# A two-stage kernel on one core: the norms and the first four MLP features moved from between the stages into the scan bodies and the second MLP chunk

## The chip, the core and the metric

One core of a Trainium2 chip runs the kernel. The engines are TensorE (PE, with its weight load PEld), VectorE (DVE), ScalarE (ACT), GpSimd (POOL) and SyncE (SP), which here only issues DMAs. Each has its own queue, taken in order, and they wait for one another by semaphores. The metric is the device time of one execution in microseconds.

## The reference

Input x is (4, 128, 128, 128): four images of 128 channels and 16384 positions.

```python
# layer 0: group norm, layer norm, Mamba over 16384 positions, residual
x1 = x + swap(mamba(layernorm(gn(x)), ...))     # W_in, conv of 4 taps, silu, delta = softplus, scan over
                                                # 16 states per channel (256 channels), y*silu(z), W_out
# layer 1, on the group norm of x1
f = lrelu(sw1 @ gn(x1) + sb1)   # 128 -> 64
f = lrelu(sw2 @ f + sb2)        # 64 -> 32
f = sw3 @ f + sb3               # 32 -> 16
# for each of 128 depth points: the 16 features and the point go through 17 -> 32 -> 32 -> 16 -> 1
sdf = sigmoid(mw4 @ lrelu(mw3 @ lrelu(mw2 @ lrelu(mw1 @ [f, point]))))   # (4, 128, 128, 128)
out = x1 + sdf
```

The group norm has 32 groups of 4 channels and takes mean and variance over whole images, so layer 1's norm of an image needs all of that image's x1.

## The kernel before

An image is cut into T = 32 tiles of L = 512 positions, NT = 128 tiles in all. All data is float32.

**Scan stage.** Loop `layer0(i)`, a "body" for each tile i from 0 to 127, and one more, number 128, that only finishes tile 127. A body has 16 units m, each a group of states. On each engine the body is a hand-written order over m:
- TensorE: `spread` of unit m + 2 (L510), which waits for the scan of unit m; at fixed m also the z, convolution and centring matmuls of tiles i + 1 and i + 2; `add_states` 0 to 2 at m = 7, 9, 12 (L521) and the fourth in the next body at m = 1; `project_out` of tile i - 1 at m = 8 (L534).
- ScalarE: `decay` of unit m + 2 (L811, Exp, two passes), `keep_last` (L815), at fixed m the silus, softplus and copies for tile i + 1; at m = 15 `diagonals` (L801, 16 passes).
- VectorE: `scan` of unit m (L1094, two passes); `gate` of tile i - 1's second half at m = 3 (L1102, L1105), of tile i's first half at m = 12; `residual` of tile i - 1 at m = 11 (L1110 and its statistics L1112); `aggregate1` of an image's statistics (L1116).
- GpSimd: `times_c` of unit m (L942), the product with C, and three diagonal tiles.
- SP: replicates C (L307) and delta (L316) over partitions, loads x, stores x1 (L289).

The group norm of the next image is worked into bodies 27, 28 and 29 of the first three images (GN_MEAN, GN_VAR, GN_SHIFT): TensorE matmuls of one column at m = 5, before `add_states` 0, which then waits for VectorE or ScalarE to have read them; VectorE's `group_dev` (L1043 to L1046) at m = 6, `group_weights` (L1051, L1053) at m = 2 and `group_bias` at m = 6; ScalarE's `group_rstd` (L722, L724) at m = 6. Image 3 has no such steps, as no image follows it.

**Between the stages.** After body 128 come, one after the other: `group_norms1` on TensorE and VectorE and `group_rstds1` on ScalarE (norms of all four images' x1); then for f = 1 to 4 the feature steps: `first_layer` for two pairs of 512-wide tiles (TensorE L620, ScalarE L868), `second_layer` (L626, L873), `third_layer` (L631), `spread_g` on VectorE (L1150, L1151). All of them use one PSUM bank, `f_ps`, so that each waits for the one before. SP loads the tiles of x1 for a feature (L354).

**MLP stage.** Loop `layer1(n)` over 128 "chunks", each of 8 steps k: `leaky1` on VectorE (L1159, 128 x 2048) makes t1 two steps ahead from g; `mm2` on TensorE (L642), `leaky2` on ScalarE (L880), for k = 1, 3, 5 partly on VectorE (L1167, L1169); `mm3` (L653), `leaky3` (L886), `mm4` (L663); a sigmoid per chunk on ScalarE (L891) at k = 3 of the next chunk; the sum with x1 on VectorE (L1176) and the store. Features 5 to 32 are made inside the chunks, one in four chunks. `leaky1` of chunk 0 waits for g of f = 4:

```python
if n % DEPTHS == 0 and k == 0:
    dve.wait_ge(s_g, GQ * (s + 1) + 1)
```

## Time and profile before

| | |
|---|---|
| runs | 9304.48, 9296.48, 9299.93 us, median 9299.93 |
| profiled execution | 9299.72 us, its span 9297.9 us |
| PE busy | 8821.4 us, 95% |
| DVE busy | 8554.3 us, 92% |
| ACT busy | 8027.6 us, 86% |
| POOL busy | 5789.4 us, 62% (all of it in the scan stage) |
| scan stage | to about 5946 us |
| MLP stage | from about 6000 us |

Busy times are of the whole span. Matmuls are pipelined, so a busy PE is not PE at its peak. PEclk is the TensorE clock that was granted, as a share of 2.4 GHz; its levels are 1 (2.4 GHz) and 0.5 (1.2 GHz). A row of the timeline has the start and the length in us, the engine, the line, the operation, its operands, how many instructions are merged in it, and in brackets the idle time before it and what ended it.

### The profile page before, as it was taken

The page shows a single profiled execution, that of the slowest core. Times are in us where ns is not written, and L with a number is a line of the kernel's source. Part 1 is how long each engine was busy: PE and PEld are TensorE (multiplying, and loading weights), DVE is VectorE, ACT ScalarE, POOL GpSimd, SP SyncE. Part 2 cuts the span into 40 slices and gives each one's busy share as a digit, 9 for nine tenths or more (in the row PEclk, how much of TensorE's full clock was granted, in tenths as well). Part 3 has the DMA queues.
Part 4 walks back from the last instruction along what each step waited for, and adds up shares of the span by engine and source line. Part 5 has one row for each costly group of instructions (what it writes and reads, how often), then busy time and mean ns, then how long its engine had stood idle before and what let it go on. Part 6 is the DMA issues. An engine that isn't in the chain of part 4 may idle for free. (4 is left out here: it accounts for less than half of the span.)

```text
span 9297.9 us, 445960 instructions
## 1 busy us (share of the span) xinstructions
PE 8821.4 (95%) x199690; PEld 3709.6 (40%) x199690; DVE 8554.3 (92%) x7167; ACT 8027.6 (86%) x12777; POOL 5789.4 (62%) x2582
## 2 busy tenths in 40 slices
PE   7999999999999999999999999799999999999999
PEld 4555555555555555555555555322222222222211
DVE  7999999999999999999999999799999999999998
ACT  6888888888888888888888888599999999999999
POOL 6999999999999999999999999500000000000000
PEclk9999999999999999999999999899999999999999
DMA  4333333333333333333333333211111111111100
GB/s 118 97 95 90 84 83 88 96 100 95 84 86 80 100 95 95 85 86 79 86 85 85 87 86 85 62 34 34 32 32 35 34 32 34 34 32 32 32 23 19
DMA packets 394196, 638.79 MB, mean 69 GB/s; under 512 B 97872, under 2 KB 98610, under 8 KB 391778
## 3 DMA queue, kind: packets, MB, share of 16 engines
q1 hardware_dynamic: 389184, 608.56, 25.0%
q8 instruction: 1577, 25.84, 1.2%
q14 instruction: 329, 2.70, 0.1%
q10 hardware_dynamic: 2498, 1.00, 0.0%
q0 software_dynamic: 608, 0.70, 0.0%
HBM read 270.13 MB, written 71.30 MB: 37 GB/s over the span
## 5 line engine op out<-in xcount | busy, mean ns | idle before, releaser
L1094 DVE TENSOR_TENSOR_SCAN arena<-arena,carried,ps 128x512 f32<-128x512 f32 x3968 | 4757.9, 1259 | 279.1 <-PE ps L510 265.1
L942 POOL TENSOR_TENSOR arena<-arena 128x1024 f32<-128x1024 f32 x2048 | 4805.1, 2404 | 87.0 <-PE ps L521 36.5
L811 ACT ACTIVATE arena<-arena,a_neg 128x512 f32<-128x512 f32 x4096 | 2662.4, 710 | 16.8 <-DVE arena L1094 10.0
L510 PE MATMUL ps<-arena 64*32 64x128 f32 x131072 | 2310.8, 276 | 74.8 <-DVE arena L1094 41.3
L1159 DVE SCALAR_TENSOR_TENSOR arena<-arena,neg_p 128x2048 f32<-128x2048 f32 x1024 | 2350.4, 2344 | 0.1
L510 PEld LDWEIGHTS ps<-arena 64*32 64x32 f32 x131072 | 1850.6, 106 | 1197.1 <-DVE arena L1094 658.5
L880 ACT ACTIVATE arena<-ps,b2t 128x1024 f32<-128x1024 f32 (+1 forms) x2048 | 2023.0, 1052 | 203.4 <-PE ps L642 203.4
L642 PE MATMUL ps<-arena,w2s 32*32 32x512 f32 x32768 | 1514.8, 599 | 105.4 <-ACT arena L880 86.2
L886 ACT ACTIVATE arena<-ps,bm 128x1024 f32<-128x1024 f32 x1024 | 1168.1, 1141 | 1.3 <-PE ps L653 1.3
L653 PE MATMUL ps<-arena,m 64*32 64x512 f32 x16384 | 1124.7, 600 | 3.6 <-ACT arena L886 0.9
L521 PE MATMUL ps<-arena,sel 128*32 128x512 f32 x8192 | 1006.5, 609 | 64.4 <-POOL arena L942 57.4
L453 PE MATMUL ps<-xnf,w_conv 128*128 128x512 f32 x2048 | 988.0, 615 | 6.6 <-issue 4.2
L642 PEld LDWEIGHTS ps<-arena,w2s 32*32 32x32 f32 x32768 | 350.4, 103 | 1215.3 <-issue 716.4
L959 POOL TENSOR_TENSOR arena<-dmask,b_t 128x1024 f32<-128x1024 f32 x384 | 744.6, 1939 | 58.7 <-ACT b_t L780 58.7
L801 ACT ACTIVATE arena<-dmask,b_t 128x64 f32<-128x64 f32 x2048 | 504.0, 341 | 99.6 <-PE ps L510 99.6
L653 PEld LDWEIGHTS ps<-arena,m 64*32 64x32 f32 x16384 | 212.8, 104 | 886.8 <-issue 886.0
L1167 DVE TENSOR_SCALAR arena<-ps,b2t 128x512 f32<-128x512 f32 x384 | 288.0, 750 | 291.3 <-PE ps L642 291.3
L663 PE MATMUL ps<-arena,m 128*32 128x512 f32 x4096 | 545.4, 605 | 1.3 <-ACT arena L886 1.3
L453 PEld LDWEIGHTS ps<-xnf,w_conv 128*128 128x128 f32 x2048 | 359.2, 190 | 395.7 <-issue 391.8
L793 ACT ACTIVATE arena<-ps 128x1024 f32<-128x1024 f32 x128 | 131.3, 1025 | 422.2 <-PE ps L494 422.2
L521 PEld LDWEIGHTS ps<-arena,sel 128*32 128x32 f32 x8192 | 220.6, 111 | 497.3 <-issue 396.9
L815 ACT ACTIVATE carried<-arena 128x4 f32<-128x4 f32 x1024 | 202.1, 197 | 245.3 <-DVE arena L1094 242.5
(136 smaller groups left out, 5840.3 us busy)
## 6 DMA issues: line engine op xcount, KB each, us to landing
arena<-arena SPq DMA_DIRECT2D x4096, 64.0 KB, 2.0
arena<-c_d SPq DMA_DIRECT2D x1024, 128.0 KB, 3.2
xr<-in_x SPq DMA_DIRECT2D x128, 256.0 KB, 3.3
x_d<-xr SPq DMA_DIRECT2D x128, 256.0 KB, 3.4
xs<-x_d SPq DMA_DIRECT2D x128, 256.0 KB, 4.3
xr<-x_d SPq DMA_DIRECT2D x128, 256.0 KB, 3.7
out<-arena SPq DMA_DIRECT2D x128, 256.0 KB, 2.4
xs<-in_x SPq DMA_DIRECT2D x96, 256.0 KB, 3.2
```

The source lines that it names most:

```text
L453: m = mm(pp[:, h, :], w_conv[:, k, h, :], xn[:, k:k + L], start=k == 0, stop=not first and k == TAPS - 1)
L510: k = mm(dst, du_t[i % 2][64 * r:64 * r + 64, c, 32 * e:32 * e + 32], diag[gp][64 * r:64 * r + 64, c, j, :], start=True, stop=True)
L521: m = mm(y_ps[32 * q:32 * q + 32, :], sel[:, :], hc[(4 * k + q) % CR][:, gi, :], start=k % 2 == 0 and gi == 0, stop=k % 2 == 1 and gi == 1)
L642: m = mm(m2_ps[32 * q:32 * q + 32, j, :], w2s[32 * j:32 * j + 32, :], t1[k % 4][32 * j:32 * j + 32, q, :], start=True, stop=True)
L653: m = mm(m3_ps[32 * j:32 * j + 32, r, :], m3[64 * r:64 * r + 64, :], t2[k % 4][64 * r:64 * r + 64, j, :], start=True, stop=True)
L811: A(dA[(UNITS * t + m) % DR][:, gi, :], drep[:, e, :], ACT.Exp, scale=a_neg[:, e, 2 * gp + gi:2 * gp + gi + 1]).then_inc(s_dA, 1)
L880: A(t2[k % 4][:, 2 * half:last, :], m2_ps[:, 2 * half:last, :], ACT.Prelu, bias=b2t[:, bias:bias + 1], alpha=SLOPE).then_inc(s_t2, 1)
L886: A(t3[k], m3_ps, ACT.Prelu, bias=bm3[:, :], alpha=SLOPE).then_inc(s_t3, 1)
L942: nc.gpsimd.tensor_tensor(hc[m % CR], H[:, m % HR, :, :], crep[:, 2 * gp:2 * gp + 2, :], ALU.mult).then_inc(s_ch, 1)
L959: d = nc.gpsimd.tensor_tensor(dst, one, col, ALU.mult)
L1094: V.tensor_tensor_scan(H[:, m % HR, gi, :], dA[(UNITS * t + m) % DR][:, gi, :], dbu[m % 2].rearrange("p (l g) -> p g l", g=2)[:, gi, :], 0 ...
L1159: V.scalar_tensor_tensor(out=t1[k % 4].rearrange("p q l -> p (q l)"), in0=g[s % 2], scalar=neg_p[:, i:i + 1], in1=gs_[s % 2], op0=ALU.max, ...
```

## The change

- The norm of x1 is split in two phases. Phase 0 takes images 0 to 2 and stands in bodies 123, 124 and 125 (tiles 27, 28, 29 of image 3) at the same m as the other group norms, in `y_ps`. Phase 1 takes image 3 and stands in MLP chunk 1 (steps k = 1 to 7) and at the start of chunk 2, in `f_ps`.
- Features 1 to 4 are made in bodies 126 and 127, in the two PSUM banks `pp`. ScalarE takes `spread_g` for these four over from VectorE. Their loads are put into SP's queue in these bodies.
- Body 128 is gone. What it did for tile 127 (the fourth `add_states`, the gate, `project_out`, the residual, its statistics and the aggregate of image 3) stands in MLP chunk 0, behind `mm2` of k = 0 and two `leaky1`.
- Feature 5's first matmuls go from step 0 to step 4 of chunk 0.
- g, f1, f2 and the output tiles get other places in the arena; a tile `gm1` is added.

```diff
-        g = [over(48 + 4 * i, 4) for i in range(2)]
+        g = [over(69, 4), over(48, 4)]
-        f1 = [over(64 + i, 1) for i in range(2)]
-        f2 = over(66, 1)
+        f1 = [over(64, 1), over(75, 1)]
+        f2 = over(77, 1)
-        ob = [over(68 + i, 1) for i in range(2)]
+        ob = [over(52 + i, 1) for i in range(2)]
+        def images(phase):
+            return slice(0, B - 1) if phase == 0 else slice(B - 1, B)
+        def first_ps(f, k):
+            return pp[:, k, :] if f <= GQ else f_ps
...
# SP, layer0
                 if real(n):
                     replicate_c(t, n % 2, 1)
+                if n == NT - 1:
+                    for f, pair in ((3, 0), (3, 1), (4, 0), (4, 1)):
+                        load_features(f, pair)
                 if real(n + 1):
                     store_c(t + 1, (n + 1) % 2)
+                if n == NT - 2:
+                    for k in range(T - XR, T):
+                        place, stored = ring(k)
+                        sp.wait_ge(s_x1[place], stored)
+                    sp.wait_ge(s_st, NT)
+                    for pair in range(2):
+                        load_features(1, pair)
...
+                if n == NT - 2:
+                    load_features(2, 0)
                 if real(n + 1):
                     replicate_c(t + 1, (n + 1) % 2, 0)
+                if n == NT - 2:
+                    load_features(2, 1)
                 if real(n + 1):
                     replicate_delta(t + 1, 1)
...
# SP, after the bodies
             sp.wait_ge(s_st1, NT + 1)
-            sp.wait_ge(s_st, NT)
-            for pair in range(2):
-                load_features(1, pair)
             for n in range(4):
                 load_x1(n)
-            for f in range(2, GQ + 2):
-                for pair in range(2):
-                    load_features(f, pair)
+            for pair in range(2):
+                load_features(GQ + 1, pair)
...
# TensorE (ScalarE has the same two functions, with spread_g for third_layer)
+            def first_features_behind(m):          # in body 126
+                if m == 11:
+                    first_layer(1, 0)
+                if m == 12:
+                    first_layer(1, 1)
+                if m == 13:
+                    second_layer(1)
+                if m == 14:
+                    third_layer(1)
+                if m == 15:
+                    for pair in range(2):
+                        first_layer(2, pair)
+            def first_features_beside(m):          # in body 127
+                if m in (3, 4):
+                    first_layer(3, m - 3)
+                if m in (10, 11):
+                    first_layer(4, m - 10)
+                for f, second, third in ((2, 0, 2), (3, 5, 6), (4, 13, 14)):
+                    if m == second:
+                        second_layer(f)
+                    if m == third:
+                        third_layer(f)
...
# TensorE, layer1
                 for k in range(NG):
+                    if first and k == 2:
+                        project_out(NT, NT - 1)
                     mm2(t, k)
+                    if first and k == 0:
+                        add_states(NT, 3)
+                    if n == 1 and k == 1:
+                        pe.wait_ge(s_f1l, 2 * (GQ + 1) + 2)
+                        group_mean1(1, f_ps[:, 0:1])
+                    if n == 1 and k == 3:
+                        group_var1(1, f_ps[:, 0:1])
+                    if n == 1 and k == 7:
+                        group_shift1(1, f_ps[:, 0:1])
...
-                        if k == 0 and part < 2:
+                        if k == (4 if first else 0) and part < 2:
                             first_layer(f, part)
...
# ScalarE
+            def spread_g(f):
+                act.wait_ge(s_gp, f + 1)
+                A(g[0][:, (f - 1) * L:f * L], first_ps(f, 1), ACT.Copy)
+                A(gs_[0][:, (f - 1) * L:f * L], first_ps(f, 1), ACT.Copy, scale=SLOPE / (1 - SLOPE)).then_inc(s_g, 1)
...
# VectorE
+            def group_dev1(phase, at):
+                n = images(phase)
+                dve.wait_ge(s_gm1, phase + 1)
+                dve.wait_ge(s_mv1, n.stop)
+                V.tensor_copy(gm1[:, n], at).then_inc(s_dev1, 1)
+                V.tensor_tensor(dev1[:, n], mv1[:, n, 0], at, ALU.subtract).then_inc(s_dev1, 1)
+                dve.wait_ge(s_dev1, 2 * phase + 2)
+                V.tensor_tensor(vd1[:, n], dev1[:, n], dev1[:, n], ALU.mult).then_inc(s_sq1, 1)
+                dve.wait_ge(s_sq1, phase + 1)
+                V.tensor_tensor(vd1[:, n], vd1[:, n], mv1[:, n, 1], ALU.add).then_inc(s_vd1, 1)
+            def group_weights1(phase):
+                n = images(phase)
+                dve.wait_ge(s_gr1, phase + 1)
+                V.scalar_tensor_tensor(out=gs1[:, n], in0=gm1[:, n], scalar=-1.0, in1=gr1[:, n],
+                                       op0=ALU.mult, op1=ALU.mult).then_inc(s_gs1, 1)
+                for b in range(n.start, n.stop):
+                    V.tensor_scalar(s1r[:, b, :], s1[:, :], gr1[:, b:b + 1], None, ALU.mult)
...
# VectorE, layer1
+                    if first and k == 1:
+                        residual(NT, NT - 1)
+                        aggregate1(NT, B - 1)
+                    if i == 1 and k == 2:
+                        group_dev1(1, f_ps[:, 0:1])
+                    if i == 1 and k == 5:
+                        group_weights1(1)
+                    if i == 2 and k == 0:
+                        group_bias1(1, f_ps[:, 0:1])
...
# VectorE, main
-            for i in range(0, NT + 1):
+            for i in range(0, NT):
                 layer0(i)
-            group_norms1()
-            for f in range(1, GQ + 1):
-                spread_g(f)
             for k in range(2):
                 leaky1(0, k)
+            gate(NT, NT - 1, 1)
```

## Rows read from the trace of the kernel before

**Rows 1.** Windows: full body 125, bodies 126, 127, gap, first MLP chunk

```profile
core 0: us, PE busy (x) PEld busy (x) DVE busy (x) ACT busy (x) POOL busy (x), PEclk, DMA share, GB/s
5798.80:5843.90 45.10, 43.02 (x1157) 23.29 (x1150) 42.77 (x39) 38.42 (x75) 45.10 (x21) 1.00 0.31 79
5843.90:5890.40 46.50, 39.43 (x1144) 22.36 (x1137) 42.15 (x39) 36.90 (x74) 45.22 (x21) 0.93 0.31 78
5890.40:5934.00 43.60, 31.59 (x1028) 19.33 (x1007) 41.73 (x38) 19.54 (x38) 42.28 (x19) 0.80 0.14 37
...
5950.00:6000.00 50.00, 32.39 (x60) 6.07 (x60) 6.09 (x14) 8.35 (x13) 0.00 (x0) 0.50 0.41 130
...
6006.00:6028.00 22.00, 21.52 (x370) 4.53 (x383) 21.90 (x15) 20.68 (x23) 0.00 (x0) 0.99 0.01 2
```

**Rows 2.** Timeline from the last scans to the first MLP matmuls

```profile
5926.89 7.13 DVE L1094 TENSOR_TENSOR_SCAN arena<-arena,carried,ps 128x512 f32<-128x512 f32 x6
...
5929.41 7.03 POOL L942 TENSOR_TENSOR arena<-arena 128x1024 f32<-128x1024 f32 x3 [1.31 <-DVE arena L1094]
...
5936.49 3.64 PE L521 MATMUL ps<-arena,sel 128*32 128x512 f32 x16 [5.95 <-POOL arena L942]
...
5946.87 1.02 DVE L1116 BATCH_NORM_AGGREGATE mv<-stats 128x2 f32<-128x192 f32 x1
...
5954.18 0.69 ACT L868 ACTIVATE arena<-ps,b1r 128x512 f32<-128x512 f32 x1 [4.08 <-PE ps L620]
...
6000.03 9.14 DVE L1159 SCALAR_TENSOR_TENSOR arena<-arena,neg_p 128x2048 f32<-128x2048 f32 x4
...
6002.43 2.02 PE L642 MATMUL ps<-arena,w2s 32*32 32x512 f32 x32 [3.83 <-DVE arena L1159]
```

**Rows 3.** Groups of instructions from 5934 to 6000.05 us

```profile
L1102 DVE SCALAR_TENSOR_TENSOR ps<-arena,dsk,ps 128x512 f32<-128x512 f32 x1 | 0.8, 755 | 6.2 <-PE ps L521 6.2
...
L1105 DVE TENSOR_TENSOR arena<-ps,arena 128x512 f32<-128x512 f32 x1 | 0.7, 691 | 0.0
```

**Rows 4.** Windows: bodies 27 to 29 of images 0, 1, 2 and 3, each summed

```profile
1310.55:1459.12 148.57, 136.62 (x3442) 73.55 (x3427) 138.78 (x124) 116.18 (x225) 135.36 (x61) 0.95 0.30 77
2775.65:2924.59 148.94, 136.70 (x3438) 74.23 (x3426) 139.22 (x124) 116.08 (x225) 135.62 (x61) 0.94 0.31 78
4238.63:4390.04 151.41, 139.12 (x3435) 75.00 (x3424) 138.78 (x124) 116.19 (x225) 135.54 (x61) 0.92 0.30 77
5708.54:5843.95 135.41, 129.88 (x3446) 70.31 (x3443) 128.19 (x118) 115.49 (x225) 135.41 (x61) 1.00 0.33 82
```

**Rows 5.** Instructions of lines L1046 and L1051: shortest, median, longest ns

```profile
L1046 DVE SCALAR_TENSOR_TENSOR vd<-dev,mv x4: 219/3910/4062, 43.6 to 4258.3; 128x1 f32<-128x1 f32 x4
...
L1051 DVE SCALAR_TENSOR_TENSOR gs<-gm,gr x4: 159/6354/6422, 45.1 to 4347.9; 128x1 f32<-128x1 f32 x4
```

**Rows 6.** Timeline where bodies 126 and 127 meet

```profile
5886.76 3.92 ACT L801 ACTIVATE arena<-dmask,b_t 128x64 f32<-128x64 f32 x16
...
5889.15 2.65 PE L510 MATMUL ps<-arena 64*32 64x128 f32 x128 [2.56 <-POOL arena L959]
5890.36 5.96 DVE L1094 TENSOR_TENSOR_SCAN arena<-arena,carried,ps 128x512 f32<-128x512 f32 x5 [0.29 <-PE ps L510]
5890.57 1.32 ACT L811 ACTIVATE arena<-arena,a_neg 128x512 f32<-128x512 f32 x2
```

**Rows 7.** Windows: MLP chunk 2, columns as in rows 1

```profile
6055.00:6080.60 25.60, 24.88 (x422) 5.34 (x422) 22.69 (x16) 24.21 (x27) 0.00 (x0) 1.00 0.17 44
```

**Rows 8.** Timeline: first loads after the residual, and the sigmoid's table load

```profile
5948.39 1.74 SPq L354 DMA_DIRECT2D xs<-x_d  x4
...
5950.17 1.85 SPq L346 DMA_DIRECT2D xr<-x_d  x4
...
5952.11 1.98 PE L620 MATMUL ps<-xs,s1r 128*64 128x512 f32 x4 [1.38 <-DMA xs<-x_d]
...
6038.68 1.28 ACT L891 ACT_TABLE_LOAD   x1
```

More of the change, by code:

```diff
@@ L115, in mamba_sdf_kernel @@
         lnv1 = sb("lnv1", [P, B])
+        gm1 = sb("gm1", [P, B])
         gr1 = sb("gr1", [P, B])
@@ L650, in mm3 @@
                 pe.wait_ge(s_t3, t * NG + k)
+                if t == 1 and k == 0:
+                    pe.wait_ge(s_yg, 2 * NT + 2)
                 for r in range(2):
@@ L692, in _ @@
             first_body()
-            for n in range(0, NT + 1):
+            for n in range(0, NT):
                 layer0(n)
-            group_norms1()
-            pe.wait_ge(s_nb1, 1)
-            for f in range(1, GQ + 1):
-                first_layer(f, 0)
-                first_layer(f, 1)
-                second_layer(f)
-                third_layer(f)
             for n in range(NT):
@@ L867, in first_layer @@
                 act.wait_ge(s_f2, f)
-                A(f1[pair], f_ps, ACT.Prelu, bias=b1r[:, b:b + 1], alpha=SLOPE).then_inc(s_f1l, 1)
+                A(f1[pair], first_ps(f, pair), ACT.Prelu, bias=b1r[:, b:b + 1], alpha=SLOPE).then_inc(s_f1l, 1)
             def second_layer(f):
@@ L872, in second_layer, with first_features_behind, first_features_beside @@
                 act.wait_ge(s_gp, f)
-                A(f2, f_ps, ACT.Prelu, bias=bs2[:, :], alpha=SLOPE).then_inc(s_f2l, 1)
+                A(f2, first_ps(f, 0), ACT.Prelu, bias=bs2[:, :], alpha=SLOPE).then_inc(s_f2l, 1)
+            def spread_g(f):
+                act.wait_ge(s_gp, f + 1)
+                A(g[0][:, (f - 1) * L:f * L], first_ps(f, 1), ACT.Copy)
+                A(gs_[0][:, (f - 1) * L:f * L], first_ps(f, 1), ACT.Copy, scale=SLOPE / (1 - SLOPE)).then_inc(s_g, 1)
+            def first_features_behind(m):
+                if m == 11:
+                    first_layer(1, 0)
+                if m == 12:
+                    first_layer(1, 1)
+                if m == 13:
+                    second_layer(1)
+                if m == 14:
+                    spread_g(1)
+                if m == 15:
+                    for pair in range(2):
+                        first_layer(2, pair)
+            def first_features_beside(m):
+                if m in (3, 4):
+                    first_layer(3, m - 3)
+                if m in (10, 11):
+                    first_layer(4, m - 10)
+                for f, second, third in ((2, 0, 2), (3, 5, 6), (4, 13, 14)):
+                    if m == second:
+                        second_layer(f)
+                    if m == third:
+                        if f == 3:
+                            act.wait_ge(s_yg, 2 * (NT - 1) + 2)
+                        spread_g(f)
             def leaky2(t, n, k, half):
@@ L898, in layer1 @@
                         sdf(t - 1)
+                    if n == 1 and k == 4:
+                        group_rstd1(1, f_ps[:, 0:1])
                     leaky2(t, n, k, 0)
@@ L905, in layer1 @@
                     if ahead:
-                        if k == 0 and part < 2:
+                        if k == (4 if first else 0) and part < 2:
                             first_layer(f, part)
@@ L915, in _ @@
             first_body()
-            for n in range(0, NT + 1):
+            for n in range(0, NT):
                 layer0(n)
-            group_rstds1()
-            act.wait_ge(s_nb1, 1)
-            for f in range(1, GQ + 1):
-                first_layer(f, 0)
-                first_layer(f, 1)
-                second_layer(f)
             for n in range(NT):
@@ L1062, in next_stats, with group_bias1 @@
                 V.bn_stats(stats[:, i, :], xs[k % SR]).then_inc(s_st, 1)
[L1064 to L1073 removed]
+            def group_dev1(phase, at):
+                n = images(phase)
+                dve.wait_ge(s_gm1, phase + 1)
[7 more added lines that the diff above has]
+            def group_weights1(phase):
+                n = images(phase)
+                dve.wait_ge(s_gr1, phase + 1)
+                V.scalar_tensor_tensor(out=gs1[:, n], in0=gm1[:, n], scalar=-1.0, in1=gr1[:, n],
                                        op0=ALU.mult, op1=ALU.mult).then_inc(s_gs1, 1)
[L1075 removed]
+                for b in range(n.start, n.stop):
                     V.tensor_scalar(s1r[:, b, :], s1[:, :], gr1[:, b:b + 1], None, ALU.mult)
[L1077 to L1078 removed]
+            def group_bias1(phase, at):
+                dve.wait_ge(s_cs1, phase + 1)
+                V.tensor_scalar(b1r[:, images(phase)], at, bs1[:, :], None, ALU.add).then_inc(s_nb1, 1)
             def normed(t, i):
```

92 lines of the change are left out of this document (60 added, 32 removed).

## Prediction

> **What bounds the kernel now.** I read the table of stages first (busy time, clock and traffic in a stretch). In the scan part VectorE is the bound: the bodies of 45.1 us hold 42.77 us of VectorE work and 45.10 us of GpSimd work [rows 1]. In the MLP part the first chunk is again VectorE's (21.90 us busy of 22.00), later chunks are a close race of TensorE and ScalarE: 24.88 and 24.21 us busy in 25.60 us, VectorE 22.69 [rows 1, 7]. Between the two lies a stretch where nobody is busy: from 5950 to 6000 us ScalarE works 8.35 us, VectorE 6.09 us, TensorE 32.39 us and that at a granted clock of 0.50, the lower of its two levels, 1.2 GHz [rows 1].
>
> The timeline then says what the stretch consists of. The last scan ends at 5934.0, GpSimd's last product at 5936.4, the last aggregate starts at 5946.87, the first MLP operation of VectorE at 6000.03 [rows 2]. So 66.0 us lie between the last scan and the first `leaky1`, a chain in which every step waits for the one before: sum of states, gate, projection, residual, norms, then four features of about 12 us each. That is all that the change can win. Of it the feature steps are short on the engines themselves (0.69 us for a ScalarE pass [rows 2]); it is the ping-pong that costs.
>
> **The change part by part.**
> 1. *The gap itself.* Removed: 66.0 us. All that follows is what comes back.
>
> 2. *The norms of images 0 to 2 inside bodies 123, 124 and 125* (body is tile; the fourth image's tiles 27, 28, 29). The same kind of chain has stood at the same places of the first three images all along, for the next image's norm, and the fourth has none. So the trace has the price. The three bodies together took 148.6, 148.9 and 151.4 us in images 0, 1 and 2, and 135.4 in image 3 [rows 4]: 13.2, 13.5 and 16.0 us more. Why so much for one-column operations: `vd` (L1046) takes 3.91 us at the median and `gs` (L1051) 6.35, where the copy of each made before GpSimd had work took 0.22 and 0.16 [rows 5]. Both read two SBUF operands while GpSimd multiplies, which is just what the new `vd1` and `gs1` do (a `tensor_tensor` of `dev1` with itself, a `scalar_tensor_tensor` of `gm1` and `gr1`), at the same steps m = 6 and m = 2 of the same two bodies. The rest is TensorE, starved behind the stall, whose granted clock over these bodies is 0.92 to 0.95 where image 3 has 1.00 [rows 4], and its wait for the logarithm in the middle body. I take 14. Bounds: 10.3 (the two stalls alone, 3.9 + 6.4) and 16. Behind the stalled VectorE stand its own scans, and behind these everything, so it counts in full.
> The Trainium skill ("SBUF — State Buffer", section "Who interferes with whom") says that a VectorE instruction with two SBUF inputs contends with a GpSimd one that reads SBUF, and that the second to issue is blocked until the first finishes. By that rule the price would be at most one GpSimd product per stall, 2.4 us, 4.8 for both, and the kernel some 5 us faster than my sum; the 6.35 us row disagrees on the length, the mechanism agrees.
>
> 3. *Features in bodies 126 and 127.* TensorE has room: in these two it works 39.43 and 31.59 us against 43.02 in a full body [rows 1], because the centring, convolution and z matmuls for later tiles are gone; the added matmuls stand where those stood. ScalarE is the one to follow. It gets 20 passes of 0.69 us (8 first-layer, 4 second-layer, 8 spreads), 13.8 us, over two bodies where it has 46.5 - 36.90 = 9.6 and 43.6 - 19.54 = 24.1 us to spare [rows 1]. But it takes them in order, waits at each for TensorE's matmul, and its next `decay` stands behind. Followed step by step in the old times: TensorE reaches third_layer(1) behind the spread of the next tile's unit 0, half of a pair that ran from 5889.15 for 2.65 us [rows 6], so at 5890.5; 1.1 us for the matmul and 1.4 for ScalarE's two copies of g make it 5893.0. Then `decay`(127, 1) 1.3 us, the 16 diagonals 3.9 us, the first layer's two passes for f = 2 1.4 us, and only then `decay`(127, 2), from 5899.6; in the profile it began at 5890.57 [rows 6]. Unit 2's scan, the fifth of five merged from 5890.36, started about 5895.1 [rows 6]; now it can start at 5900.3 (first half of the decay done). So 5.2 us of stall in VectorE, the bound. In the rest of body 127 ScalarE is 24 us idle and a step costs only if matmul, pass and the next decay take more than the two scans (4.8 us) that lie between: 1.2 + 1.1 + 1.4 + 1.3 = 5.0 for a spread, so some tenths at some steps. I take 6 for the two bodies. Bounds 2 (a spread that finds ScalarE in time) and 11 (lower clock, where the same matmuls take twice as long).
> On SP the loads of features 1 lie in a hole before the delta replication; those of f = 2 to 4 wait for a matmul, with the replication of e = 4 to 7 and of C behind them by about 2 us. These are used ten us later, so 0.
>
> 4. *From the last scan to `leaky1`(0, 0).* It needs g of f = 4. Second layer, third layer and two copies after unit 13's scan are 2.3 + 0.7 + 1.1 + 1.5 = 5.6 us, and 4.8 of these pass under scans 14 and 15: 0.8 us. But `leaky1` reads g and gs from SBUF and GpSimd is still in its last product, 2.4 us after the last scan [rows 2]. By item 2 it waits for that. I take 2.4; bounds 0.8 and 4 (lower clock).
>
> 5. *The tail of tile 127 inside MLP chunk 0.* VectorE bounds this chunk, so its added work counts in full: gate 0.76 + 0.69, residual 0.69, stats 0.69, aggregate 1.02 [rows 2, 3]: 3.85. Besides, the gate stands third in VectorE's queue, after two `leaky1` (4.6 us), and waits for `add_states`, which TensorE does only after `mm2`(1, 0). That one starts 2.4 us after the first `leaky1` and takes 2.0 at the lower clock [rows 2]; the 16 matmuls then take 1.9 to 3.64 [rows 2]: done at 7.2, a wait of 2.6. Behind it are all later `leaky1`. Then the loads: the residual ends about 15.4 us into the chunk; in the profile the first load after it was issued at 5948.39, 2.3 us after the residual, and was used at 5952.11 [rows 8]. SP now issues four tiles of x1 first (1.85 us [rows 8]) and then feature 5: 15.4 + 2.3 + 1.85 + 3.7 = 23.2, where TensorE wants it at about 22.4. 0.8 us. Sum 7.2, I take 7. Bounds: 4 (work alone) and 10 (six loads of 256 KB each queue up).
>
> 6. *The last image's norm in chunks 1 and 2.* TensorE: waits for ScalarE's pass of the first layer (0.5) and three tiny matmuls with weight loads of about 0.4 each. ScalarE: logarithm and exponential 0.26 + 0.20, and its function table must go from sigmoid's to the logarithm's and back in the next sigmoid: 2 loads of 1.28 us [rows 8], 3 if logarithm and exponential come from different tables. VectorE 1.2 us, hidden in its 2.9 us of idle per chunk [rows 7]; without that cover 1.2. TensorE and ScalarE share the bound, with 0.7 and 1.4 us spare in a chunk [rows 7], so I count ScalarE's 3.0 and TensorE's 1.7 nearly in full: 4.5. Bounds 2 and 7. The Trainium skill ("ScalarE: Activation LUTs", section "What ACT_TABLE_LOAD costs") gives 2.66 us for a switch with its drain; by that this item would be 2.8 us more; the load in the trace lasts 1.28.
>
> Sum: 66.0 - 14 - 6 - 2.4 - 7 - 4.5 = 32.1 us. The profiled execution took 9299.7 us (span 9297.9), the median shown is 9299.9, so the two agree: 9299.7 - 32.1, about 9268. With every term at its cheap bound 66.0 - 19.1 gives 9253; at its dear bound 66.0 - 48 gives 9282. Of what a measurement can tell, 0.2% is 18.6 us.
>
> **The rivals.**
> - *The stalls of VectorE do not repeat* (a `tensor_tensor` behaves unlike the `scalar_tensor_tensor` of before, or GpSimd happens to be idle) or last one product only: 5 to 12 us more gain, 9256 to 9263. For it: VectorE's operation is another one. Against: of three stalls of either kind the longest is within 0.15 us of the median [rows 5].
> - *ScalarE becomes the bound of bodies 126 and 127.* Ten hand-overs, each 1.8 us late (spread and matmul at the lower clock, 0.80 was granted in body 127 [rows 1]) beside the 5.2: 23 us instead of 6, 9285, within 0.2% of before. It decides from 1.3 us at each. Against: after unit 2 ScalarE has 24 us to spare.
> - *Function tables alternate in bodies 126 and 127*, as Prelu stands among Exps: about ten switches there and back at 1.28 us, 26 us, 9294. Against: the first Prelu in the gap comes at 5954.18 after 4.08 us in which ScalarE had nothing, no load either, and what stood before that was the norm's Exp [rows 2].
> - *Slower:* the MLP loop settles into another rhythm, since VectorE now enters it late and g and the output tiles lie elsewhere. There are 126 more chunks of 25.6 us; 0.4 us on each is 50 us, 9318. It decides from there: below 0.4 us the kernel is not slower by 0.2%. Against: TensorE's work fills the chunks, not the order of entry.
>
> **How the numbers follow.** My sum 0.66; no or shorter stalls 0.14; ScalarE as bound 0.09; tables 0.03; other rhythm 0.04; and 0.04 for a gain beyond all bounds. The middle three lie within or at the edge of 0.2%, and a twentieth of the first case may end below 18.6 us: faster 0.85, same 0.11, slower 0.04. The range from 9251 to 9284 takes the first two cases and a part of the third.
>
> **What the profile after would show.** Bodies 123 to 125 of some 149 us together, with `vd1` near 4 and `gs1` near 6 us. A VectorE wait of 4 to 5 us on `decay` before unit 2 of body 127. The first `leaky1` 2.4 us after the last scan, at about 5956. A second aggregate in chunk 0, a TensorE wait on a load before first_layer(5, 0). Two or three table loads in chunks 1 and 2, then the old 25.6 us. Most likely to be wrong: the size of item 3, where one hand-over missed delays a whole body, and item 5's wait on the loads.

## The result, and the profile after

The changed kernel takes 9268.92 us (median of 7 runs, 9263.21 to 9276.60), the kernel before 9296.48 us (median of 7, 9289.03 to 9311.57). The ratio is 0.997 with a 95% interval of 0.996 to 0.998, so it is faster by 27.6 us. The prediction was 9268, its range 9251 to 9284. It forecast a gain of 32.1 us from 9299.7; the kernel before, run four more times, has a median 3.45 us lower than the one that stood there, so the time was met more closely than the gain. The profiled execution after took 9273.04 us, its span is 9271.2.

The first view is again the table of stages. It shows bodies 123 to 125 together, then bodies 126 and 127, 10 us from the first `leaky1` on, the MLP chunks 0 to 3, each from its first `leaky1` to the next chunk's, and at the end the 10 us around the last image's logarithm:

```profile
core 0: us, PE busy (x) PEld busy (x) DVE busy (x) ACT busy (x) POOL busy (x), PEclk, DMA share, GB/s
5712.63:5860.88 148.25, 134.62 (x3438) 72.99 (x3428) 139.57 (x127) 116.18 (x225) 135.71 (x61) 0.95 0.27 75
5860.88:5906.02 45.14, 40.93 (x1139) 22.43 (x1123) 42.00 (x39) 34.16 (x59) 45.14 (x21) 0.96 0.43 121
5906.02:5953.05 47.03, 39.50 (x1072) 18.70 (x1071) 41.86 (x38) 32.60 (x71) 42.57 (x19) 1.00 0.28 84
...
5953.68:5963.68 10.00, 6.04 (x64) 1.17 (x80) 6.54 (x3) 2.12 (x2) 1.75 (x1) 0.50 0.00 0
...
5953.68:5986.02 32.34, 23.79 (x304) 4.73 (x304) 27.49 (x19) 16.25 (x17) 1.75 (x1) 0.79 0.25 82
5986.02:6017.73 31.71, 27.87 (x428) 5.87 (x424) 23.71 (x22) 29.27 (x33) 0.00 (x0) 0.90 0.01 2
6017.73:6046.43 28.70, 26.56 (x450) 5.80 (x458) 23.16 (x17) 26.12 (x28) 0.00 (x0) 0.99 0.13 39
6046.43:6072.86 26.43, 25.46 (x448) 5.17 (x431) 24.14 (x19) 24.30 (x26) 0.00 (x0) 1.00 0.14 42
...
6007.70:6017.70 10.00, 8.55 (x100) 1.37 (x104) 5.21 (x7) 9.27 (x12) 0.00 (x0) 0.70 0.01 2
```

What the reader is to see, against [rows 1, 4, 7]: the 50 us in which no engine filled its time are gone. The three bodies that took 135.41 us take 148.25. Bodies 126 and 127 took 46.50 and 43.60 at clocks of 0.93 and 0.80; they now take 45.14 and 47.03 at 0.96 and 1.00, with the feature matmuls in them. The MLP starts at the lower clock, and its first three chunks are longer than the 22.27, 26.20 and 25.95 us that the same stretches, cut by the same rule, took before.

The timeline (start, length, instructions, in brackets the idle time before and what ended it) shows the places that the prediction named. First the two stalls of the norm and what GpSimd did at the time, then the point in body 127, then the start of the MLP:

```profile
5720.07 16.29 POOL L1057 TENSOR_TENSOR arena<-arena 128x1024 f32<-128x1024 f32 x7
...
5732.29 4.08 DVE L1186 TENSOR_TENSOR vd<-dev 128x3 f32<-128x3 f32 x1
...
5817.72 7.00 POOL L1057 TENSOR_TENSOR arena<-arena 128x1024 f32<-128x1024 f32 x3
...
5818.29 6.44 DVE L1193 SCALAR_TENSOR_TENSOR gs<-gm,gr 128x3 f32<-128x3 f32 x1
...
5824.66 0.57 DVE L1196 TENSOR_SCALAR s1r<-s,gr 128x64 f32<-128x64 f32 x3
...
5915.33 0.20 ACT L895 ACTIVATE carried<-arena 128x4 f32<-128x4 f32 x1
...
5915.73 4.79 DVE L1216 TENSOR_TENSOR_SCAN arena<-arena,carried,ps 128x512 f32<-128x512 f32 x4 [4.51 <-ACT carried L895]
...
5948.40 7.03 POOL L1057 TENSOR_TENSOR arena<-arena 128x1024 f32<-128x1024 f32 x3 [1.29 <-DVE arena L1216]
...
5953.68 6.16 DVE L1288 SCALAR_TENSOR_TENSOR arena<-arena,neg_p 128x2048 f32<-128x2048 f32 x2 [0.67 <-ACT arena L964]
...
5959.59 3.64 PE L544 MATMUL ps<-arena,sel 128*32 128x512 f32 x16
...
5963.30 0.75 DVE L1224 SCALAR_TENSOR_TENSOR ps<-arena,dsk,ps 128x512 f32<-128x512 f32 x1 [3.46 <-PE ps L544]
...
5982.27 1.08 PE L667 MATMUL ps<-xs,s1r 128*64 128x512 f32 x4 [1.82 <-DMA xs<-x_d]
...
6004.52 1.28 ACT L1010 ACT_TABLE_LOAD   x1
...
6009.11 1.28 ACT L808 ACT_TABLE_LOAD   x1
6010.40 0.26 ACT L808 ACTIVATE lnv<-ps,epsc 128x1 f32<-128x1 f32 x1
6010.68 1.28 ACT L810 ACT_TABLE_LOAD   x1
```

Both stalls end at the moment at which GpSimd's row of back-to-back products ends: 5732.29 + 4.08 = 5736.37 against 5720.07 + 16.29 = 5736.36, and 5818.29 + 6.44 = 5824.73 against 5817.72 + 7.00 = 5824.72. The last scan ends at 5953.01 and `leaky1` starts at 5953.68, where 66.0 us lay before. The fourth table load of these chunks, the next sigmoid's, stands at 6036.28.

### The profile page after: what moved, and what is told of

Same layout as the page of the kernel before. It is cut to its first block and busy times, and to the rows that moved or that the text cites. A ratio compares the mean times of both kernels' runs of the same rounds, so it can differ in the third digit from the quotient of the medians.

```text
span 9271.2 us, 446057 instructions
## 1 busy us (share of the span) xinstructions
PE 8803.9 (95%) x199698; PEld 3701.4 (40%) x199698; DVE 8562.9 (92%) x7166; ACT 8039.4 (87%) x12789; POOL 5791.7 (62%) x2582
```

## The experiments

Each kernel starts from the changed one and computes the same. All but c1 and c2 ran once. The kernel before took 9302.00 us beside e1a to e3, 9297.16 (median of 9) beside e4 to c2, and 9297.02 beside p1. Its single runs lie up to 22 us apart, so a single edit is judged by the length of the stage that it touches, each from the table of stages. Chunk n is the time from its first `leaky1` to the next chunk's.

| kernel | time us | bodies 123 to 125 | 126 + 127 | chunk 0 | chunk 1 | chunk 2 |
|---|---|---|---|---|---|---|
| before | 9296.48 | 135.41 | 90.10 | 22.27 | 26.20 | 25.95 |
| changed | 9268.92 | 148.25 | 92.17 | 32.34 | 31.71 | 28.70 |
| e1a, one SBUF input | 9277.22 | 146.59 | 92.44 | 33.67 | 33.10 | 28.56 |
| e1b, weights on ScalarE | 9260.77 | 139.69 | 93.66 | 32.66 | 32.78 | 31.38 |
| e2, norm before sigmoid | 9267.45 | 148.75 | 92.20 | 32.73 | 29.95 | 27.94 |
| e3, feature 5 first | 9264.52 | 147.28 | 92.36 | 31.63 | 32.50 | 30.97 |
| e4, states first | 9268.22 | 147.35 | 92.36 | 28.87 | 32.49 | 30.51 |
| e5, later hand-over | 9275.83 | 152.10 | 92.22 | 31.83 | 32.50 | 30.58 |
| c1, all of e1b to e5 | 9250.95 | 139.83 | 90.70 | 30.08 | 30.14 | 27.47 |
| c2, c1 and the older norms | 9220.39 | 139.53 | 92.19 | 28.49 | 30.14 | 27.42 |
| p1, ten probes | 9314.18 | 151.05 | 92.20 | 33.13 | 32.50 | 30.91 |

Most fields belong to stages that the edit of their row leaves alone. They show how far one and the same code spreads from one execution to the next:
- Bodies 123 to 125 take 147.28 to 152.10 us (the changed kernel, e2, e3, e4, e5, p1).
- Bodies 126 and 127 take 92.17 to 92.44 us together, and 93.66 in e1b.
- Chunk 0 takes 31.83 to 33.67 us (the changed kernel, e1a, e1b, e2, e5, p1).
- Chunks 1 and 2 together take 60.41 us in the changed kernel, 63.08 in e5 and 63.41 in p1. In chunk 2 the granted clock is 0.99 in the first and 0.91 in the other two.

A difference inside such a spread is not the effect of an edit.

**e1a: no VectorE operation of two SBUF operands in the norm.** The square goes through PSUM, and `gs1` is made column by column with a scalar operand.

```diff
-                V.tensor_tensor(vd1[:, n], dev1[:, n], dev1[:, n], ALU.mult).then_inc(s_sq1, 1)
+                V.tensor_tensor(dev_ps, mv1[:, n, 0], at, ALU.subtract).then_inc(s_dev1, 1)
+                V.tensor_tensor(sq_ps, dev_ps, dev1[:, n], ALU.mult).then_inc(s_sq1, 1)
...
-                V.scalar_tensor_tensor(out=gs1[:, n], in0=gm1[:, n], scalar=-1.0, in1=gr1[:, n],
-                                       op0=ALU.mult, op1=ALU.mult).then_inc(s_gs1, 1)
+                for b in range(n.start, n.stop):
+                    v = V.tensor_scalar(gs1[:, b:b + 1], gm1[:, b:b + 1], gr1[:, b:b + 1], -1.0, ALU.mult, ALU.mult)
+                v.then_inc(s_gs1, 1)
```

> The norm steps of bodies 123 and 125 on VectorE with at most one SBUF tensor input each: the deviation is also written to PSUM and squared from there, the variance is added to the PSUM square, and gs is three tensor_scalar operations with the rstd as a scalar. Same engine, same places, same semaphore chain. Theory A (the 4.08 and 6.44 us in the changed kernel are the wait of a two-SBUF-input operation for GpSimd to run dry): both disappear, each operation takes 0.15 to 0.25 us, the three bodies go from 148.3 to about 137 to 139 us. Rival B (the stall comes from the chain of tiny operations and semaphores at that place, or any SBUF operation waits): the stalls stay near 4 and 6 us, perhaps on another operation of the chain, and the bodies stay at 148. If only the tensor_scalar stalls, gs or s1r takes 6 us and the bodies 144.

Timeline of e1a:

```profile
5735.46 0.17 DVE L1189 TENSOR_TENSOR ps<-ps,dev 128x3 f32<-128x3 f32 x1
...
5818.40 0.43 DVE L1197 TENSOR_SCALAR gs<-gm,gr 128x1 f32<-128x1 f32 x3
5818.75 6.45 DVE L1200 TENSOR_SCALAR s1r<-s,gr 128x64 f32<-128x64 f32 x3
```

The square takes 0.17 us instead of 4.08, in the middle of a row of GpSimd's of 18.74 us, and body 123 takes 45.12 us, where it took 50.1 to 51.3 in the changed kernel, e2 to e5 and p1. The sum behind it (L1191) reads one SBUF and one PSUM operand, writes to SBUF and takes 0.16 us, so a result in SBUF alone does not bring the wait. The three `gs1` take 0.43 us together. But the wait went to the next instruction, `s1r`, which took 0.57 us when it stood behind the stalled `gs1` and now takes 6.45, though it reads one SBUF tile and a scalar column. So half of the theory stands (the square's stall comes of its two SBUF operands), and half falls: an operation with one larger SBUF operand waits as well. VectorE is busy for 3.9 us less, the square's stall. The three bodies together take 146.59 us, 0.7 below the spread of the changed code, so their own gain cannot be told from this one execution.

**e1b: VectorE does no weights.** As e1a, and `gs1` and `s1r` are ScalarE copies with a scale, one step earlier.

```diff
+            def group_weights1(phase):          # ScalarE
+                n = images(phase)
+                act.wait_ge(s_gr1, phase + 1)
+                for b in range(n.start, n.stop):
+                    A(s1r[:, b, :], s1[:, :], ACT.Copy, scale=gr1[:, b:b + 1])
+                    v = A(gs1[:, b:b + 1], gm1[:, b:b + 1], ACT.Copy, scale=gr1[:, b:b + 1])
+                v.then_inc(s_gs1, 1)
```

> As the run before, but the weights (gs and s1r) of both phases are made by ScalarE: six passes of about 0.2 us at m = 1 of body 125. Theory A (two SBUF inputs under GpSimd): no stall in either, 137 to 139 us for the three bodies, equal to the run before within 1 us. If a one-input tensor_scalar from SBUF to SBUF also waits for GpSimd, this run is 4 to 6 us shorter in body 125 than the run before. Rival B (tiny chains as such): vd still near 4 us.

Table of stages of e1b, bodies 123 to 125:

```profile
5703.31:5843.00 139.69, 133.17 (x3443) 72.19 (x3433) 129.25 (x123) 116.89 (x231) 135.53 (x61) 0.98 0.29 80
```

VectorE is busy for 129.25 us instead of 139.57 (the two stalls are 10.5), and the bodies are 8.6 us shorter, at a clock of 0.98 instead of 0.95. c1 and c2, which have the same repair, take 139.83 and 139.53 us; the unrepaired code takes 147.28 to 152.10, so the repair is worth 7.5 to 12.6 us. Against the 135.41 us without a norm 4.3 us are left; the single waits of the norm that these are made of were not tried one by one. So of the norm's 12.8 us in the changed kernel's trace two thirds were the two stalls.

**e2: the last image's logarithm before the sigmoid**, so that the sets of functions change in one place.

```diff
-                    if k == 3 and not first:
+                    if k == 3 and n > 1:
                         sdf(t - 1)
                     if n == 1 and k == 4:
                         group_rstd1(1, f_ps[:, 0:1])
+                        sdf(t - 1)
```

> In MLP chunk 1 ScalarE makes the first sigmoid at step 4, right after the last image's logarithm and exponential, instead of at step 3 ahead of them. In the changed kernel there are four table loads in chunks 1 and 2 (sigmoid, logarithm, exponential, sigmoid again). Theory: the table that the scan bodies left holds both functions, so only one load (sigmoid) stays, 3.85 us of loads go, and chunks 1 and 2 together shrink by 3.5 to 5 us, since ScalarE has little slack there. Rival: chunks 1 and 2 are long because of TensorE's tiny matmuls and waits; then they shrink by less than 1 us.

Timeline of e2:

```profile
6004.05 0.27 ACT L808 ACTIVATE lnv<-ps,epsc 128x1 f32<-128x1 f32 x1
6004.35 0.20 ACT L810 ACTIVATE gr<-lnv 128x1 f32<-128x1 f32 x1
6004.57 1.28 ACT L1010 ACT_TABLE_LOAD   x1
```

Only the load at 6004.57 is left of the four: with the table of the scan bodies still in place, logarithm and exponential need none. Chunks 1 and 2 take 57.9 us, and 57.6 in c1 and c2, which have the same edit. The kernels without it take 60.4 to 64.2. So the edit wins 2.5 us or more, where three loads of 1.28, 3.84 us, are gone; whether it wins the 3.5 to 5 that were expected this spread does not tell. In chunk 1 ScalarE is busy for 26.85 us instead of 29.27.

**e3: feature 5's loads in SP's queue before the stores of x1 and the four tiles of x1.**

```diff
+                if n == NT:
+                    for pair in range(2):
+                        load_features(GQ + 1, pair)
                 if real(n - 1):
                     store_x1(n - 1)
...
             for n in range(4):
                 load_x1(n)
-            for pair in range(2):
-                load_features(GQ + 1, pair)
```

> SP issues the loads of feature 5 before the last x1 tile is stored and before the first x1 tiles are loaded. In the changed kernel TensorE waits 1.82 us in chunk 0 for that load. Theory (the wait is on the path): the wait goes and chunk 0 shrinks by 1.5 to 2 us. Rival (VectorE bounds chunk 0, and the wait fell into time that TensorE had to spare): the wait goes but the start of chunk 1 moves by less than 0.5 us.

The wait of 1.82 us for the load is gone: `first_layer`(5, 0) starts at 5968.84. Chunk 0 takes 31.63 us, 0.7 less than in the changed kernel and 0.2 less than in e5. Chunks 1 and 2 take 63.47 us, as in p1 (63.41), where nothing was edited. But the wait comes and goes without the edit too: with the loads in the old order it is 1.20 us in e1a, and e1b, e2, e4, e5 and p1 have no wait that is put down to a load there. So this run cannot tell what the edit is worth; no gain shows beyond the spread.

**e4: the fourth `add_states` before `mm2`(1, 0).**

```diff
                     if first and k == 2:
                         project_out(NT, NT - 1)
-                    mm2(t, k)
                     if first and k == 0:
                         add_states(NT, 3)
+                    mm2(t, k)
```

> In MLP chunk 0 TensorE sums the last states of tile 127 before its first mm2 instead of behind it. In the changed kernel VectorE waits 3.46 us for that sum with the gate, and all later leaky1 stand behind the gate. Theory (this wait is on the path, as VectorE bounds chunk 0): the wait shrinks to under 0.5 us, the first mm2 starts some 1.5 us later, and chunk 0 is 2.5 to 3.5 us shorter. Rival (chunk 0 is bound by TensorE and by the load of feature 5, and VectorE only waits in another place): chunk 0 changes by less than 1 us.

Timeline and, below, chunks 0 to 2 of e4:

```profile
5951.17 3.58 PE L544 MATMUL ps<-arena,sel 128*32 128x512 f32 x16 [3.02 <-POOL arena L1057]
...
5955.45 0.74 DVE L1224 SCALAR_TENSOR_TENSOR ps<-arena,dsk,ps 128x512 f32<-128x512 f32 x1
```

```profile
5949.37:5978.24 28.87, 23.22 (x304) 4.83 (x304) 27.40 (x20) 16.11 (x17) 1.75 (x1) 0.88 0.27 92
5978.24:6010.73 32.49, 27.10 (x428) 5.89 (x424) 23.71 (x22) 29.49 (x33) 0.00 (x0) 0.92 0.01 2
6010.73:6041.24 30.51, 28.35 (x450) 5.97 (x457) 23.15 (x17) 26.27 (x28) 0.00 (x0) 0.91 0.12 36
```

The gate has no wait in its brackets any more, and chunk 0 takes 3.5 us less than in the changed kernel, which is the wait of 3.46 there, and 3.0 less than 31.83, the shortest chunk 0 with neither this edit nor e3's. Chunks 1 and 2 take 63.00 us, 2.6 more than in the changed kernel, with TensorE's clock in chunk 2 at 0.91 instead of 0.99. This looks as if the gain were given back, but it is not an effect of the edit: p1 has 63.41 us and 0.91 there with the very code of the changed kernel, and e5, whose edit lies in other stages, 63.08 and 0.91. What makes the clock of chunk 2 0.91 in one execution and 0.99 in another no run shows. With e2's edit, in e2, c1 and c2, it was 0.96 and 0.98.

**e5: the hand-overs of features 1 to 3 one step later**, with feature 1's spread behind the diagonals.

```diff
-                if m == 15:
-                    for pair in range(2):
-                        first_layer(2, pair)
...
-                if m in (3, 4):
-                    first_layer(3, m - 3)
+                if m == 1:
+                    for pair in range(2):
+                        first_layer(2, pair)
+                if m in (4, 5):
+                    first_layer(3, m - 4)
...
-                for f, second, third in ((2, 0, 2), (3, 5, 6), (4, 13, 14)):
+                for f, second, third in ((2, 2, 3), (3, 6, 7), (4, 13, 14)):
```

> ScalarE's two spread passes of feature 1 and the first layer of feature 2 go from the end of body 126 to units 0 and 1 of body 127, behind decay of unit 2 and the carried states; feature 2's and 3's later steps come one unit later. Nothing else changes. Theory (the 4.51 us wait of VectorE before unit 2 of body 127 is ScalarE's queue: spread, decay, 16 diagonals, two passes, decay, carried states): it shrinks to under 1 us and bodies 126 and 127 together go from 92.2 to 88 to 89 us. Rival (TensorE's spread behind the added matmuls is what is late): the wait moves to a release by TensorE and the sum stays above 91 us.

Timeline of e5 and its bodies 126 and 127:

```profile
5913.36 4.79 DVE L1216 TENSOR_TENSOR_SCAN arena<-arena,carried,ps 128x512 f32<-128x512 f32 x4 [1.57 <-ACT carried L895]
```

```profile
5860.33:5906.95 46.62, 42.56 (x1139) 23.17 (x1133) 42.12 (x38) 34.41 (x61) 45.24 (x21) 0.93 0.41 117
5906.95:5952.55 45.60, 39.36 (x1072) 18.62 (x1071) 41.75 (x38) 32.56 (x70) 42.43 (x19) 1.00 0.30 88
```

VectorE's wait before unit 2 is 1.57 instead of 4.51 us, and body 127 is 1.4 us shorter. It takes 45.6 us in all three kernels with this edit (e5, c1, c2) and 47.0 to 47.3 in the others. Body 126 is 1.5 us longer at a clock of 0.93, so the sum does not move here: 92.22 against 92.17 us, where 88 to 89 were expected. That the missing feature 2 matmuls at its end cost the clock is not shown: c1 has the same edit and takes 45.11 us in body 126 at a clock of 1.00 (both bodies 90.70), and e1b, which has these matmuls in the old place, takes 46.64 us at 0.93.

**p1: what makes a VectorE instruction wait for GpSimd.** Ten instructions whose results nobody uses, one in each of bodies 100 to 109, at a given step m.

```diff
+                    # body: (m, kind, columns)
+                    probes = {100: (2, 0, 3), 101: (5, 0, 3), 102: (9, 0, 3), 103: (14, 0, 3), 104: (2, 1, 1),
+                              105: (2, 1, 3), 106: (2, 1, 64), 107: (2, 2, 64), 108: (2, 2, 1), 109: (2, 0, 64)}
+                        if kind == 0:
+                            V.tensor_tensor(o, v, v, ALU.mult)
+                        elif kind == 1:
+                            V.tensor_scalar(o, v, bs1[:, :], None, ALU.mult)
+                        else:
+                            V.tensor_copy(o, v)
```

> The changed kernel with one extra small VectorE operation, whose result nobody reads, in each of bodies 100 to 109. tensor_tensor of two SBUF inputs, 3 columns, before the scan's successor at m = 2, 5, 9 and 14 (bodies 100 to 103); tensor_scalar with one SBUF input and 1, 3 and 64 columns at m = 2 (104 to 106); tensor_copy from SBUF of 64 and of 1 column at m = 2 (107, 108); tensor_tensor of 64 columns at m = 2 (109). Theory A (the operation waits until GpSimd's row of back-to-back products ends, that is for its whole backlog): about 6.4 us at m = 2, 4 us near m = 6, and each ends within 0.1 us of the end of a GpSimd row; the 64-column tensor_scalar and copy wait as long, those of 1 column take 0.15 us. Theory B (it waits for the one GpSimd operation that runs): none takes over 2.5 us.

Timeline of p1, the probes and GpSimd at the first and the fourth:

```profile
4673.32 6.98 POOL L1058 TENSOR_TENSOR arena<-arena 128x1024 f32<-128x1024 f32 x3
...
4673.86 6.45 DVE L1253 TENSOR_TENSOR probe<-s 128x3 f32<-128x3 f32 x1
...
4859.32 1.90 POOL L1075 TENSOR_TENSOR arena<-dmask,b_t 128x1024 f32<-128x1024 f32 x1
4859.82 1.43 DVE L1253 TENSOR_TENSOR probe<-s 128x3 f32<-128x3 f32 x1
4861.18 4.70 POOL L1058 TENSOR_TENSOR arena<-arena 128x1024 f32<-128x1024 f32 x2
...
4871.96 0.19 DVE L1255 TENSOR_SCALAR probe<-s,bs 128x1 f32<-128x1 f32 x1
...
4916.91 5.77 DVE L1255 TENSOR_SCALAR probe<-s,bs 128x3 f32<-128x3 f32 x1
...
5017.78 6.44 DVE L1257 COPY probe<-s 128x64 f32<-128x64 f32 x1
5071.06 0.13 DVE L1257 COPY probe<-s 128x1 f32<-128x1 f32 x1
```

The product of two SBUF operands with 3 columns took 6.45, 4.13, 6.18 and 1.43 us at m = 2, 5, 9 and 14. The first three end where GpSimd's row of work ends (4673.86 + 6.45 = 4680.31 against 4673.32 + 6.98 = 4680.30). The fourth ends with one single GpSimd operation (4861.25 against 4861.22), while GpSimd goes on. It is the only one that began during one of GpSimd's diagonals (L1075); the others began during a product with C (L1058). A `tensor_scalar` of 3 or 64 columns waits (5.77, 6.37 us), so do a copy and a product of 64 (6.44 and 5.54 us), but a `tensor_scalar` or a copy of a single column does not (0.19, 0.13). So it is not the kind of operation and not its second operand alone. Why the wait is one GpSimd operation at m = 14 and a whole row elsewhere stays open. The ten probes together last 42.6 us, and bodies 100 to 109 take 491.6 us instead of the 455.7 of the changed kernel (453.4 to 459.3 in the other kernels): most of such a wait, but not all of it, reached the length of the bodies.

**c1: all of e1b, e2, e3, e4 and e5.** The diffs are those above.

> All parts together on the changed kernel: one SBUF input in vd, weights by ScalarE, sigmoid behind the norm, feature 5 loaded first, states first, later hand-over. If the parts add up as measured or expected one by one: 8.5 + 2.5 + 0.7 + 3 + 3.5 = 18 us below the changed kernel, about 9251. If they hide each other or the clock falls elsewhere, 8 to 12 us below it.

9250.95 us (5 runs, 9245.60 to 9253.08), 0.9947 of before with an interval of 0.9934 to 0.9959. That is 18.0 us below the changed kernel, as the sum of the parts had it (18). By stages 8.4 us come from the norm (8.5 expected), 1.5 from bodies 126 and 127 (3.5 expected), and 5.1 from chunks 0 to 2 (87.69 against 92.75 us; 6.2 expected from e2, e3 and e4). These are 15.0 us; the rest of the 18.0 lies in code that is the same in both. So the total was met with luck, and two of the parts came out smaller.

**c2: c1, and the same for the norms that were in the kernel all along.**

```diff
+            def group_weights(b):               # ScalarE
+                act.wait_ge(s_gr, b + 1)
+                A(cen_r[:, b % 2, :], cen[:, :], ACT.Copy, scale=gr[:, 0:1])
+                A(gs[:, :], gm[:, :], ACT.Copy, scale=gr[:, 0:1]).then_inc(s_gs, 1)
...
-                V.scalar_tensor_tensor(out=vd[:, :], in0=dev[:, :], scalar=dev[:, :], in1=mv[:, 1:2],
+                V.scalar_tensor_tensor(out=vd[:, :], in0=dev_ps, scalar=dev[:, :], in1=mv[:, 1:2],
```

> As the run before, and the layer 0 norms of images 1 to 3 in bodies 27 to 29 of the first three images get the same form: the deviation through PSUM, gs and the scaled centring matrix by ScalarE. Theory (the price of these bodies, 13.2, 13.5 and 16.0 us over three plain ones, is for the larger part the wait of VectorE for GpSimd): 8 to 10 us less in each of the three images, 24 to 30 us below the run before. Rival (the price is TensorE's wait for norm results at m = 7 and its clock): less than 3 us in each.

Bodies 27 to 29 of images 0, 1 and 2 in c2, and of image 0 in c1:

```profile
1306.30:1444.16 137.86, 131.57 (x3445) 71.45 (x3433) 128.61 (x123) 116.19 (x228) 135.48 (x61) 0.99 0.32 85
...
2761.63:2900.99 139.36, 133.56 (x3441) 72.21 (x3428) 128.64 (x123) 116.10 (x227) 135.32 (x61) 0.98 0.32 83
...
4213.56:4351.31 137.75, 131.68 (x3439) 71.54 (x3430) 128.74 (x123) 116.10 (x227) 135.50 (x61) 0.99 0.32 85
```

```profile
1311.39:1464.20 152.81, 140.69 (x3434) 75.14 (x3423) 138.17 (x123) 116.11 (x224) 135.44 (x61) 0.92 0.28 76
```

In c1 the three images' bodies took 152.81, 148.91 and 146.89 us, so c2 wins 15.0, 9.6 and 9.1, 33.6 us in all. The same three of the changed kernel took 151.98, 151.91 and 149.26. The old norm's `vd` takes 0.22 us in c2 each time, where it took 3.91 at the median [rows 5]: one of its operands now comes from PSUM. It takes 9220.39 us (5 runs, 9212.08 to 9227.30), 30.6 below c1 and 0.9916 of before (0.9903 to 0.9930). It is the fastest kernel here. Taking the stalls out of the three old norms was thus worth more than the whole change (27.6 us).

## Why the prediction was right, term by term

| term | predicted us | in the profile us |
|---|---|---|
| 1, gap | -66.0 | -66.0 |
| 2, norms in bodies 123 to 125 | 14 | 148.25 - 135.41 = 12.8 |
| 3, features in 126 and 127 | 6 | 92.17 - 90.10 = 2.1 |
| 4, start of `leaky1` | 2.4 | 0.67 + 1.55 = 2.2 |
| 5, tail of tile 127 in chunk 0 | 7 | 32.34 - 22.27 - 1.55 = 8.5 |
| 6, last norm in chunks 1 and 2 | 4.5 | 5.5 + 2.8 = 8.3 |
| sum | -32.1 | -32.1 |

The sum is met to a tenth because errors of both signs cancel: item 3 was 3.9 too high and item 2 1.2, items 5 and 6 together 5.3 too low. That is luck, and it belongs to this one execution. In p1, which has the same code in these stages, items 2, 5 and 6 come to 36.2 us in place of 29.6, as bodies 123 to 125 and chunks 0 to 2 are 6.6 us longer.

The span itself fell by 26.7 us. The rest is in code that the change does not touch: body 123 begins at 5712.63 instead of 5708.54 (4.1), and from chunk 3 to the end it takes 3224.8 instead of 3223.5 us (1.3). The lengths of the first 123 bodies differ as much between the kernels with the same code there (5621.7 to 5635.5 us), so this is no effect of the change.

*Item 2 was right in mechanism and size.* (In p1 it comes to 15.6 us.) The row of the old norm priced the new one: 4.08 and 6.44 us against 3.91 and 6.35 in [rows 5], and e1b, which takes both stalls away, gives 8.6 of the 12.8 us back. That a stall counts in full was a little too strong: in e1b 10.3 us less of VectorE's time made the bodies 8.6 us shorter, in p1 42.6 us of probes made them 35.9 longer. The rival that the stalls do not repeat or last one product is out for this place. On this the Trainium skill ("SBUF — State Buffer", "Who interferes with whom") says that the second of two contending instructions is blocked until the first finishes. At 4.08 and 6.44 us the trace disagrees on the length, except for the 1.43 us at m = 14 of p1. The same section says that an instruction with at most one SBUF input does not contend outside the modes that use two ports, and that a copy or a `tensor_scalar` can enter these; e1a's square (0.17 us) and `s1r` (6.45 us) agree with both.

*Item 3 had the right place and order and was mis-sized.* The stall before unit 2 of body 127 was 4.51 us, 5.2 predicted. It is released by `keep_last` and not by half of the `decay`: 5915.33 + 0.20 = 5915.53, and the scan starts at 5915.73. What was missed has the other sign. Before, TensorE fell to 0.93 and 0.80 in these bodies [rows 1]; with the features in them it has 0.96 and 1.00. In body 127 VectorE idled for 1.9 us before; of its 5.2 now 4.5 are the stall, so 1.2 us of other waits are gone. Body 126, for which the sum allowed no gain, became 1.4 us shorter. The higher clock in body 127 holds in every kernel with the features (0.96 or 1.00). The shorter body 126 does not: in e1b it takes 46.64 us at 0.93. The prediction took the lower clock only as a danger for the added matmuls, not as a cost of before that they would remove. The rival that ScalarE bounds these bodies is out, as is the one of alternating function tables: the last table load of these bodies begins at 5883.47, before the first feature pass, and the next one is in chunk 1, at 6004.52.

*Item 4 was right.* The last copy of g ends 0.6 us after the last scan, 0.8 predicted. The first two `leaky1` take 6.16 us instead of 4.6, and GpSimd's last product ends at 5948.40 + 7.03 = 5955.43, 2.4 us after the last scan, as predicted. The first `leaky1` is held until about then. With 0.67 us before it that is 2.2 in place of 2.4. The wait is inside the instruction's own length, where no row of waits shows it.

*Item 5 was mis-sized in its waits.* The gate waits 3.46 us, not 2.6, since the 16 matmuls of `add_states` took 3.64 us at the lower clock (0.50 in these 10 us), the dear end of the 1.9 to 3.64 given; e4 takes this wait away and chunk 0 becomes 3.5 us shorter. TensorE's wait on the load is 1.82 us, not 0.8; but five other kernels with the same loads do not show it, and chunk 0 takes 31.83 to 33.13 us in four of them (e1b, e2, e5, p1) as against 32.34, so it did not set the chunk's length. The fifth is e4, with its own edit in the chunk.

*Item 6 was the worst.* 8.3 us instead of 4.5, beyond its dear bound of 7. There are four table loads in chunks 1 and 2 where one stood before: logarithm and exponential load a set each, which the prediction had left open between 2 and 3 extra loads, and priced with about 3.0 us of ScalarE in all where three loads alone are 3.84. e2 shows 2.5 us or more of it. The other part goes with TensorE's clock: it waits 1.68 us for `leaky2` behind the first load and 1.45 behind the next two, and over the 10 us from 6007.70 on the granted clock is 0.70. The prediction had no term for it. In p1 the same code costs 11.3 us here, with a clock of 0.91 in chunk 2 instead of 0.99, so the size depends on the execution. How much of it is the clock alone was not separated.

*The slower rival, another rhythm of the MLP loop, is out.* Chunk 3 takes 26.43 us, and chunk 3 to the end is 1.3 us of 3224 longer. The changed place of g and of the output tiles costs nothing that shows.

## What to carry to other kernels

A step that is moved costs what the same step already costs where it stands in the trace: look for its twin before working a price out, and then ask whether the twin itself can be made cheaper, which was here worth more (30.6 us) than the change (27.6 us). A tiny VectorE instruction beside a busy GpSimd can cost 4 to 6 us; put such work on ScalarE, or through PSUM. Read the stages that an edit does not touch as well. Here the same code took 3 us more or less in two chunks, and up to 4.8 in three bodies, from one execution to the next. A gain that seems to be given back next door may be no more than this, and only a kernel that shares the code there can tell.

## What the runs showed of the hardware that was not expected

- A VectorE `tensor_scalar` or copy of 3 or 64 columns in SBUF waits for GpSimd like an operation of two SBUF operands (5.77, 6.37 and 6.44 us in p1), while one on a single column takes 0.19 and 0.13 us.
- The wait mostly lasts until GpSimd has run out of queued work, over up to three operations (in both places of the changed kernel and in seven of the eight waits of p1 the two ends agree within 0.1 us), but once ended after one operation with more work right behind it (1.43 us at m = 14). What decides is not known.
- After a sigmoid, a logarithm and an exponential right behind it load a table each (6009.11 and 6010.68, 1.28 us each). The Trainium skill ("ScalarE: Activation LUTs", "Table sets: the hidden batching unit") says that a logarithm followed by an exponential needs one load, as one set has both. The trace disagrees on the count, though e2 bears out that one set can serve both: there neither loads one behind the scan bodies. The same page gives 2.66 us for a switch with its drain ("What ACT_TABLE_LOAD costs"); here the logarithm starts at 6010.40, 0.01 us after the end of the load.
- The same code can get another TensorE clock in another execution. In MLP chunk 2 it was 0.99 in the changed kernel (28.70 us) and 0.91 in p1 (30.91 us) and e5 (30.58 us). Why is not known.
